# A graph network on one core: batch norm and gate on turned tiles, row norms tile by tile, a second feature buffer, and the start of the build

## The chip, the core and the metric

One core of a Trainium2 chip runs the whole network. The metric is the device time of one execution in microseconds (us). The kernel is written in Bass: every engine has its own program, and the engines meet only at semaphores. TensorE is PE, VectorE is DVE, ScalarE is ACT, GpSimd is POOL and SyncE is SP.

## What is computed

A graph has 3125 nodes with 96 features (`x`) and 100,000 directed edges (`src`, `dst`). Four blocks are added to `x`, each after a layer norm and a ReLU:

```python
h = relu(layernorm(x)); x = x + L0(h)   # two graph convolutions, batch norm and sigmoid between them
h = relu(layernorm(x)); x = x + L1(h)   # two SAGE layers: h @ W_self + mean_of_neighbours(h) @ W_neigh + b
h = relu(layernorm(x)); x = x + L2(h)   # two attention layers with graph norms
h = relu(layernorm(x)); x = x + L3(h)   # degree-normalised sum over edges
# L0
h = graph_conv(h)                        # segment_sum((h * out_norm)[src], dst) * in_norm + bias1
h = sigmoid(batch_norm(h, gamma, beta))  # mean and variance of each feature over the nodes
h = graph_conv(h)                        # same, with bias2
```

## The kernel before, in words

The nodes are 25 tiles of 128 (`NT`), in five groups of five (`G`, `NG`). The kernel first builds the dense adjacency matrix of edge counts, 3200 x 3200 in fp16 (`ADJ`), and every sum over edges is then a matrix product with it.

**The build (`build_adjacency`, L145 to L555).** The edges are sorted by destination. DVE compares sampled destinations with 196 bounds in four slices (L304), PE adds the comparisons up (L399), and DVE makes of them 196 start addresses (L309). Packed edge keys are written to DRAM (L240, L492) and come back as 196 short windows, one DMA each, in seven loads of 8, 16, 28 and four times 36 windows. `load_windows` (L133) reads the addresses from SBUF into registers, four at a time (`QUAD`), and issues the DMAs. SP and ACT each issue half of loads 0 and 1; SP issues all others; a load waits until the buffer it goes to was turned. ACT then issues the loading of `x` (L499, L500). For every four windows (a quad, 49 of them) DVE makes one-hot rows and codes (L331, L338) and ACT a fifth part of the codes (L513, L521). PE multiplies them (L428), ACT stores the counts (L535), and PE adds degrees (L438). PE turns the keys of the next load (L412) after the third-last quad of a load (after the first one of load 0), in its own order between the products, and DVE unpacks them (L317) after the second-last quad (the last one of load 0). Beside the stores of pairs 8 to 32, ACT also takes the sum and the squared deviation of each tile of `x` (L541, L542) for the first layer norm.

**A sum over edges (`pe_aggregate`, L594).** The features stand in `k.Y` as two fp16 halves (high and low, 192 columns). A pass has 625 products of 128 x 128 by 192 columns. The first five output tiles are summed together in five PSUM banks, group of sources by group as `y_ready` comes; then tile after tile with 25 products each, each waiting until its bank was read. `after(j)` puts further PE work behind tile j. DVE reads a bank by adding the two halves (L620).

**The stages around the change, all in `convolutions` and `sage`:** the first layer norm is applied (L730 to L742); the sums of layer 1 (with column sums of `H` by PE, L693); batch norm and gate: mean (L771), centring (L773), squares by ACT (L831), column sums of squares by PE (50 products, L693), scale (L781) and shift (L788) in DVE passes over all tiles, sigmoid by ACT (L836), a multiply by POOL (L816), then the high and low halves (L631, L637); the sums of layer 2; the second layer norm: for each group the sum, mean, centring (L646 to L648), square (L656), sum of squares (L662), and, after the last group, one square root and a pass over all five groups (L669 to L680); the SAGE sums with two turns (L1009, L1010) and two small products (L1018, L1019) after each tile, and the weights scaled by DVE (L917 to L922) before its first bank is read; ReLU by ACT (L982), halves, the second SAGE sums, and the third layer norm in the same way as the second. `attention_weights` turns small weights on PE and DVE between the two stages. `prepare_attention` then turns `H` again (L1269, L1242).

```python
for v, y_ready, w in ((s, k.y_ready, w1), (u, u.y_ready, w2)):     # sage, PE
    after = step(v, w)
    pe_aggregate(k, nc, pe, v, y_ready, 1, ONE, after)
    after(NT)
    after(NT + 1)
```

## Time and profile before

| | before |
|---|---|
| median of 3 runs | 943.2 us (941.07 to 944.72) |
| the profiled execution | 944.32 us, span 942.5 us |
| mean granted clock of TensorE, as a share of full speed | 0.895 |
| PE, PEld, DVE, ACT, POOL busy | 741.9, 674.9, 650.9, 470.6, 10.5 us |
| build, up to the first product of the sums (L598) | 0 to 214.02 us |
| layer 1 sums; batch norm and gate | to 274.49; to 302.69 us |
| layer 2 sums; second layer norm | to 357.87; to 365.82 us |
| SAGE 1 sums; change to SAGE 2; its sums | to 439.76; to 444.71; to 514.17 us |
| first product of the attention's preparation | 523.71 us |
| attention, norms and the last sum, which the change leaves alone | to 942.5 us |

Times are from the start of the span. The span is 1.8 us shorter than the device time of the same execution. A matmul is pipelined, so that its listed duration (250 ns) is longer than the distance to the next one. The clock is the share of full speed that was granted: 1.00 is 2.4 GHz and 0.50 is 1.2 GHz.

### The profile page before, as it was taken

The numbers are of one execution on the slowest core, as the hardware profiler recorded it, in microseconds if no ns is written. First come the engines' busy times: TensorE is split into PE (matmuls) and PEld (weight loads), VectorE is DVE, ScalarE is ACT, GpSimd is POOL, SyncE is SP. The second block draws the span as 40 slices with busy tenths as digits, with TensorE's granted clock in tenths as the row PEclk, the third lists the DMA queues.
The fourth block names the chain that finished last, engine by engine and source line by source line (L and its number), as shares of the span: only waits on it lengthen the run. The fifth ranks groups of instructions, "written<-read, shape, count | busy, mean of one in ns | idle before, by whom it ended". The sixth has DMA issues, their size and how long they took to land. (4 is left out here: it accounts for less than half of the span.)

```text
span 942.5 us, 20574 instructions
## 1 busy us (share of the span) xinstructions
PE 741.9 (79%) x8051; PEld 674.9 (72%) x8051; DVE 650.9 (69%) x1513; ACT 470.6 (50%) x937; POOL 10.5 (1%) x19
## 2 busy tenths in 40 slices
PE   3776888869984996898999749998753999880598
PEld 2555655549974996898999649888642988770498
DVE  5888999974346445334444769998866999889632
ACT  1899999861013002112111559888554988760200
POOL 1000000000002000000000000000000000000000
PEclk8898999998986998999999559999955999995699
DMA  2200000006950000000000210000001489918501
GB/s 74 62 11 11 9 6 2 1 8 239 413 237 1 1 1 1 2 1 2 1 2 11 95 32 16 16 16 2 1 1 33 90 184 190 173 39 229 119 23 31
DMA packets 95284, 56.17 MB, mean 60 GB/s; under 512 B 87960, under 2 KB 89418, under 8 KB 94792
## 3 DMA queue, kind: packets, MB, share of 16 engines
q1 hardware_dynamic: 93982, 52.65, 20.3%
q10 hardware_dynamic: 1194, 2.06, 0.7%
q8 instruction: 69, 1.13, 0.5%
q14 instruction: 39, 0.32, 0.1%
HBM read 9.26 MB, written 24.97 MB: 36 GB/s over the span
## 5 line engine op out<-in xcount | busy, mean ns | idle before, releaser
L598 PE MATMUL banks<-y_sb,adjacency 128*128 128x192 f16 (+1 forms) x2500 | 227.9, 252 | 30.3 <-DVE y_sb L637 30.3
L598 PEld LDWEIGHTS banks<-y_sb,adjacency 128*128 128x128 f16 x2500 | 220.7, 101 | 32.1 <-DVE y_sb L637 30.9
L428 PE MATMUL counts<-hot_code,hot_row 128*128 128x100 f16 (+3 forms) x1568 | 122.1, 219 | 38.1 <-ACT hot_code L521 19.5
L428 PEld LDWEIGHTS counts<-hot_code,hot_row 128*128 128x128 f16 x1568 | 93.5, 101 | 77.8 <-DVE hot_code L338 32.9
L1701 PE MATMUL banks<-loose,y_sb 128*128 128x194 f16 x540 | 101.4, 251 | 0.0
L620 DVE TENSOR_REDUCE h_sb<-banks 128x96 f32<-128x192 f32 x75 | 26.7, 356 | 105.0 <-PE banks L598 67.0
L1700 PE MATMUL banks<-x_sb,gat_masks 128*128 128x194 f16 x420 | 79.8, 252 | 23.3 <-DVE gat_masks L1625 15.3
L338 DVE TENSOR_TENSOR hot_code<-codes_iota,unpacked 128x600 f16<-128x600 f16 x196 | 96.8, 555 | 0.0
L1700 PE MATMUL banks<-x_sb,y_sb 128*128 128x194 f16 x400 | 75.2, 250 | 13.9 <-DVE h_sb L1625 9.9
L535 ACT ACTIVATE adjacency<-counts 128x800 f16<-128x800 f32 x98 | 81.2, 828 | 10.0 <-PE counts L428 9.9
L1673 ACT ACTIVATE gat_masks<-y_sb,node_scalars 128x640 bf16<-128x640 f32 x84 | 68.1, 825 | 29.6 <-PE banks L1701 17.3
L331 DVE TENSOR_TENSOR hot_row<-rows_iota,unpacked 128x2560 f16<-128x2560 f16 x49 | 72.6, 1482 | 7.7 <-PE counts L428 7.6
L1700 PE MATMUL banks<-x_sb,h_sb 128*128 128x194 f16 x430 | 75.8, 247 | 0.8
L1920 PE MATMUL banks<-y_sb,adjacency 128*128 128x192 f16 x625 | 55.0, 252 | 27.0 <-DVE y_sb L637 27.0
L1920 PEld LDWEIGHTS banks<-y_sb,adjacency 128*128 128x128 f16 x625 | 54.4, 100 | 27.9 <-issue 27.5
L978 ACT ACTIVATE loose<-banks 96x256 f32<-96x256 f32 x50 | 19.0, 379 | 110.3 <-PE banks L1010 110.2
L1701 PE MATMUL banks<-loose,h_sb 128*128 128x194 f16 x400 | 72.4, 247 | 0.0
L1673 ACT ACTIVATE y_sb<-y_sb,node_scalars 128x640 bf16<-128x640 f32 x80 | 65.0, 825 | 10.6 <-PE banks L1701 9.7
L1673 ACT ACTIVATE h_sb<-y_sb,node_scalars 128x640 bf16<-128x640 f32 x86 | 68.2, 824 | 0.7 <-PE banks L1701 0.3
L620 DVE TENSOR_REDUCE loose<-banks 128x96 f32<-128x192 f32 x50 | 17.8, 356 | 72.9 <-PE banks L598 72.9
L1700 PEld LDWEIGHTS banks<-x_sb,gat_masks 128*128 128x128 f16 x420 | 41.7, 99 | 29.4 <-DVE gat_masks L1619 16.9
L513 ACT ACTIVATE distance<-codes_iota,negative 128x100 f16<-128x100 f16 x196 | 57.5, 368 | 4.6 <-issue 4.2
(230 smaller groups left out, 1233.8 us busy)
## 6 DMA issues: line engine op xcount, KB each, us to landing
kept_adj<-adjacency SPq DMA_DIRECT2D x5, 4000.0 KB, 32.0
y_sb<-a_dst_rows SPq DMA_DIRECT2D x10, 320.0 KB, 3.5
window_keys<-edge_keys SPq DMA_DIRECT2D x184, 5.0 KB
kept_x<-x_sb SPq DMA_DIRECT2D x1, 1200.0 KB, 4.3
residual<-h_sb SPq DMA_DIRECT2D x5, 240.0 KB, 2.1
loose<-residual SPq DMA_DIRECT2D x1, 1200.0 KB, 5.3
x_sb<-kept_x SPq DMA_DIRECT2D x1, 1200.0 KB, 8.0
out_x<-x_sb SPq DMA_DIRECT2D x4, 240.0 KB
```

The lines of the kernel that those rows point to most:

```text
L331: dve.tensor_tensor(hot_row[:, h, :, :].rearrange("p n (a b) -> p n a b", b=2), rows_iota[:, :].rearrange("p (a b) -> p a b", b=2).unsquee ...
L338: dve.tensor_tensor(hot_codes(h, b).rearrange("p w (a b) -> p w a b", b=2), codes_iota[:, FROM[b]:FROM[b] + WIDE[b]].rearrange("p (a b) -> ...
L428: last = nc.tensor.matmul(counts[:, 2 * (p % HELD) + i, start:end], hot_row[:, q % 2, b * QUAD + w, :], hot_codes(q % 2, b)[:, w, start - ...
L513: nc.scalar.activation(distance[:, q % 2, w, :], codes_iota[:, FROM[-1]:CODES], ACT.Abs, bias=negative[:, load % 2, at:at + 1]).then_inc(d ...
L535: nc.scalar.activation(k.ADJ[:, :, 2 * p * W:2 * (p + 1) * W].rearrange("p t (b o) -> p t b o", o=W), counts_of(2 * (p % HELD), 2), ACT.Co ...
L598: return nc.tensor.matmul(k.ps[:, j % G, 0:cols], k.ADJ[:, i, j * P:(j + 1) * P], k.Y[:, i, 0:cols], start=i == 0, stop=i == NT - 1)
L620: return nc.vector.tensor_reduce(out, k.ps[:, b, 0:ONE].rearrange("p (q f) -> p f q", q=PARTS), axis=AX, op=ALU.add)
L978: nc.scalar.activation(HT[:, j % 2, :], k.ps[0:C, TURNED, 0:2 * P], ACT.Copy).then_inc(v.copied, 1)
L1673: nc.scalar.activation(step_of(x), row[ch % 2], ACT.Relu, bias=k.a_s5[:, i:i + 1], scale=STEEP).then_inc(t.step_ready, 1)
L1700: nc.tensor.matmul(bank[:, 0:2 * BC], over_of(x)[:, q * P:(q + 1) * P], features[0][:, i, :], start=i == 0, stop=False)
L1701: return nc.tensor.matmul(bank[:, 2 * BC:4 * BC], under_of(x)[:, q * P:(q + 1) * P], features[1][:, i, :], start=False, stop=i == NT - 1)
L1920: return nc.tensor.matmul(k.ps[:, j % BANKS, 0:ONE], k.ADJ[:, a * G + i % G, at:at + P], k.Y[:, i, 0:ONE], start=i == 0, stop=i == NT - 1)
```

## The change

In the build: `x` is loaded by SP in six DMAs before the codes are written out; DVE measures each tile with `bn_stats` (five tiles before it turns the counts into start addresses, twenty after); ACT's statistics go; registers are filled up to twelve at a time; ACT issues the last four windows of loads 0 and 1, SP the others; PE multiplies `bound` by itself 60 times before its counting and 45 times after it, into a bank that is overwritten later.

Batch norm: PE turns tiles of `H` between the sums of layer 1, DVE measures the turned tiles in PSUM with `bn_stats`, scale and shift are then columns, and ACT reads the turned tiles and gives the sigmoid of all in one instruction a group; PE turns the gates back, DVE multiplies them with `out_norm`. Row norms: after each tile of the sums DVE takes `bn_stats` and `bn_aggr` of that row tile, and ACT applies the norm and the ReLU with a scale and a bias per row. SAGE 1 reads its features from `k.Y2`, which lies in `k.loose`, and writes those of SAGE 2 to `k.Y` while it sums. The weights of the attention are turned in the batch norm stage. POOL clears the build's semaphores beside the later work.

```diff
+ADDRESSES = 12
+BY_ACT = 4
+STATS_FIRST = 5
+BUSY_FIRST, BUSY_NEXT = 60, 45
 def load_windows(nc, k, d, eng, engine, load, keys, windows, landed):
-    for at in range(0, len(windows), QUAD):
-        some = windows[at:at + QUAD]
+    for at in range(0, len(windows), ADDRESSES):
+        some = windows[at:at + ADDRESSES]
...
+        sp.wait_ge(x_pad, 1)
+        for g in range(NG):
+            full = min((g + 1) * G, NT - 1)
+            sp.dma_start(k.X[:, g * G:full, :], d.x[g * G * P:full * P, :].rearrange("(t p) f -> p t f", p=P)).then_inc(x_in, 16)
+        sp.dma_start(k.X[0:LAST, NT - 1, :], d.x[(NT - 1) * P:N, :]).then_inc(x_in, 16)
         sp.wait_ge(codes_ready, 1)
...
-                         windows[:len(windows) // 2] if load < 2 else windows, window_in[load])
+                         windows[:len(windows) - BY_ACT] if load < 2 else windows, window_in[load])
...
-        dve.wait_ge(count_ready, 1)
-        dve.tensor_scalar(k.start_i[:, :], count_ps, float(STEP), None, ALU.mult).then_inc(starts_ready, 1)
+        dve.wait_ge(x_in, 16 * (NG + 1))
+        for t in range(NT):
+            if t == STATS_FIRST:
+                dve.wait_ge(count_ready, 1)
+                dve.tensor_scalar(k.start_i[:, :], count_ps, float(STEP), None, ALU.mult).then_inc(starts_ready, 1)
+            last = dve.bn_stats(node_stats[:, t, :], k.X[:, t, :])
...
+        pe.wait_ge(iotas, 1)
+        keep_busy(BUSY_FIRST)
         for s in range(SLICES):
...
         last.then_inc(count_ready, 1)
+        keep_busy(BUSY_NEXT)
...
-                chain(nc.scalar.activation(centred, k.X[:, t, :], ACT.Copy, scale=1.0 / C, accum_out=k.mean0[:, t:t + 1]))
-                nc.scalar.activation(squared, k.X[:, t, :], ACT.Square, scale=-1.0, bias=k.mean0[:, t:t + 1],
-                                     accum_out=k.var0[:, t:t + 1]).then_inc(mean_ready, 1)
```

The rest of the core, of `pe_aggregate`, the row norm, `convolutions` and `sage`:

```diff
     for g in range(NG):
         pe.wait_ge(y_ready, g + 1)
         for j in range(G):
+            if g == 0 and drained is not None:
+                pe.wait_ge(drained, NT - G + j + 1)
...
+        if between is not None:
+            between(g)
...
+def row_statistics(nc, k, dve, s, j):
+    dve.wait_ge(s.added, j + 1)
+    if j >= 2:
+        dve.wait_ge(s.row_moments, j - 1)
+    dve.bn_stats(k.row_stats[:, j % 2, :], k.X[:, j, :]).then_inc(s.row_measured, 1)
+def row_moments(nc, k, dve, s, j):
+    dve.wait_ge(s.row_measured, j + 1)
+    dve.bn_aggr(k.moments[:, j, :], k.row_stats[:, j % 2, :]).then_inc(s.row_moments, 1)
+def row_variance(nc, k, dve, s, g):
+    dve.wait_ge(s.row_moments, G * (g + 1))
+    dve.tensor_scalar(group(k.row_dev, g), tiles(k.moments, g)[:, :, 1], LN_EPS, None, ALU.add).then_inc(s.variance, 1)
+def row_scales(nc, k, dve, s, g):
+    dve.wait_ge(s.deviation, g + 1)
+    dve.reciprocal(group(k.row_scale, g), group(k.row_dev, g)).then_inc(s.row_scale, 1)
+    dve.wait_ge(s.row_scale, g + 1)
+    nc.vector.scalar_tensor_tensor(out=group(k.row_shift, g), in0=tiles(k.moments, g)[:, :, 0], scalar=-1.0,
+                                   in1=group(k.row_scale, g), op0=ALU.mult, op1=ALU.mult).then_inc(s.row_shift, 1)
+def act_row_deviation(nc, k, act, s, g):
+    act.wait_ge(s.variance, g + 1)
+    nc.scalar.activation(group(k.row_dev, g), group(k.row_dev, g), ACT.Sqrt).then_inc(s.deviation, 1)
+def act_normalise_rows(nc, k, act, s, g):
+    act.wait_ge(s.row_shift, g + 1)
+    for t in range(g * G, (g + 1) * G):
+        nc.scalar.activation(k.H[:, t, :], k.X[:, t, :], ACT.Relu, scale=k.row_scale[:, t:t + 1],
+                             bias=k.row_shift[:, t:t + 1]).then_inc(s.normal, 1)
...
+BN_TURN_AT = ((8, 0, 5), (13, 5, 10), (18, 10, 12), (22, 12, 16), (23, 16, 20))
+BN_MEASURE_AT = (10, 15, 20, 24)
...
+            for j in range(first, end):
+                nc.vector.scalar_tensor_tensor(out=k.H[:, j, :], in0=k.H[:, j, :], scalar=k.in_norm[:, j:j + 1], in1=bias,
+                                               op0=ALU.mult, op1=ALU.add).then_inc(s.h_ready, 1)
...
+        for n in range(len(BN_MEASURE_AT), NC + 1):
+            measure(nc, k, dve, s.tiles_turned, s.measured, n)
+        dve.wait_ge(s.columns, 2 * 16)
+        dve.wait_ge(s.measured, NC + 1)
+        chain(dve.bn_aggr(k.columns[:, 2:4], k.column_stats.rearrange("p n e -> p (n e)")))
...
         for g in range(NG):
+            dve.wait_ge(s.back, g + 1)
+            dve.tensor_tensor(tiles(k.H, g), back(g), across(group(k.out_norm, g)), ALU.mult).then_inc(u.value, 1)
...
+        for j in range(NT + 6):
+            if j < NT:
+                dve.wait_ge(u.summed, j + 1)
+                add_parts(nc, k, tiles(k.H, j, 1), j % G).then_inc(u.emptied, 1)
+            if 0 <= j - 1 < NT:
+                update(j - 1)
+            if 0 <= j - 2 < NT:
+                row_statistics(nc, k, dve, u, j - 2)
+            if 0 <= j - 3 < NT:
+                row_moments(nc, k, dve, u, j - 3)
+            if (j - 3) % G == G - 1 and 0 <= j - 3 < NT:
+                row_variance(nc, k, dve, u, (j - 3) // G)
+            if (j - 4) % G == G - 1 and 0 <= j - 4 < NT:
+                row_scales(nc, k, dve, u, (j - 4) // G)
+            if (j - 6) % G == G - 1 and 0 <= j - 6 < NT - G:
+                dve_low(nc, k, dve, (j - 6) // G, u.next_high, u.next_y, k.Y2)
+        dve_low(nc, k, dve, NG - 1, u.next_high, u.next_y, k.Y2)
...
+                gate = nc.scalar.activation(gates[:, g % 2, (first - g * G) * P:(first - g * G) * P + z - a],
+                                            flat(k.ps[0:C, :, :])[:, a:z], ACT.Sigmoid, scale=scale, bias=shift)
+        act.preload_act_table(ACT.Sqrt)
         for g in range(NG):
+            act_row_deviation(nc, k, act, u, g)
+            act_normalise_rows(nc, k, act, u, g)
+            act.wait_ge(u.normal, G * (g + 1))
+            act_high(nc, k, g, u.next_high, k.Y2)
...
+            if j == 0:
+                weights()
             if j >= 2:
                 output_1(j - 2)
+            if BIASED_FROM <= j < BIASED_FROM + NG:
+                g = j - BIASED_FROM
...
+                dve.tensor_tensor(tiles(k.X, g), tiles(k.X, g), down(b2[:, :], G), ALU.add).then_inc(s.biased, 1)
+            if j >= 2 * G and j % G == 0:
+                dve_low(nc, k, dve, j // G - 2, s.high, u.y_ready, k.Y)
+        dve_low(nc, k, dve, NG - 1, s.high, u.y_ready, k.Y)
...
+            act.wait_ge(s.relu, g + 1)
+            act_high(nc, k, g, s.high, k.Y)
...
+        act_row_deviation(nc, k, act, u, NG - 1)
+        act_normalise_rows(nc, k, act, u, NG - 1)
...
+        first, second = step(s, w1), step(u, w2)
+        pe_aggregate(k, nc, pe, s, k.Y2, k.y_ready, 1, ONE, first, k.drained)
+        pe_aggregate(k, nc, pe, u, k.Y, u.y_ready, 1, ONE, second, s.emptied, lambda g: first(NT + g) if g < 2 else None)
+        second(NT)
+        second(NT + 1)
```

## Rows read from the trace of the kernel before

**Rows 1.** Stretches by stage: PE, PEld, DVE, ACT, POOL busy, clock, DMA share, GB/s.
```profile
60.00:100.00 40.00, 27.85 (x329) 22.71 (x327) 31.22 (x49) 39.45 (x133) 0.00 (x0) 0.83 0.05 11
100.00:201.60 101.60, 87.58 (x1100) 60.30 (x1097) 101.50 (x159) 92.79 (x213) 0.00 (x0) 1.00 0.02 4
...
274.49:302.69 28.20, 11.48 (x61) 10.82 (x61) 16.11 (x28) 9.39 (x17) 6.20 (x5) 0.68 0.00 0
302.69:357.87 55.18, 55.18 (x628) 54.85 (x629) 25.86 (x52) 3.16 (x6) 0.00 (x0) 0.95 0.01 1
357.87:365.82 7.95, 0.38 (x6) 0.29 (x5) 6.81 (x14) 3.29 (x5) 0.00 (x0) 0.83 0.00 0
365.82:378.40 12.58, 12.58 (x127) 12.37 (x127) 5.40 (x15) 1.81 (x3) 0.00 (x0) 0.84 0.00 1
378.40:384.78 6.38, 3.39 (x23) 2.80 (x22) 4.33 (x17) 1.72 (x5) 0.00 (x0) 0.91 0.01 3
...
439.76:444.71 4.95, 2.39 (x19) 1.92 (x18) 2.09 (x7) 3.20 (x7) 0.00 (x0) 1.00 0.01 3
444.71:456.95 12.24, 12.24 (x127) 12.03 (x127) 6.24 (x11) 1.22 (x3) 0.00 (x0) 0.86 0.00 1
```

**Rows 2.** Groups by line, 31 to 202 us: busy, mean ns, idle before, releaser.
```profile
L331 DVE TENSOR_TENSOR hot_row<-rows_iota,unpacked 128x2560 f16<-128x2560 f16 x47 | 69.7, 1482 | 7.7 <-PE counts L428 7.6
```

**Rows 3.** Timeline of the build's first 32 us: start, duration, idle before.
```profile
8.09 3.62 DVE L304 TENSOR_TENSOR adjacency<-bound,sample 125x1568 f16<-125x1568 f16 x4
...
9.12 5.38 PE L399 MATMUL degree_ps<-adjacency,ones_h 125*1 125x196 f16 x32 [9.12 <-DVE adjacency L304]
...
31.03 0.32 DVE L317 CAST unpacked<-keys_ps 128x160 f16<-128x160 f32 x1 [4.23 <-PE keys_ps L412]
```

**Rows 4.** Two stretches: key writes (8 to 11.6 us) and the load of x.
```profile
8.00:11.60 3.60, 2.48 (x16) 1.95 (x17) 3.60 (x5) 0.00 (x0) 0.00 (x0) 1.00 0.70 222
...
24.00:28.50 4.50, 0.04 (x3) 0.01 (x1) 2.80 (x5) 1.77 (x6) 0.00 (x0) 0.50 0.90 264
```

**Rows 5.** Timeline of window and x issues, and PE's turn of load 2.
```profile
15.70 22.39 SPq L142 DMA_DIRECT2D window_keys<-edge_keys  x40
...
23.45 3.14 ACTq L500 DMA_DIRECT2D x_sb<-in_x  x1
...
40.31 0.51 PE L412 MATMUL keys_ps<-ident,window_keys 56*128 56x56 f32 x5
```

**Rows 6.** Line 137, register loads of four addresses: ns min/median/max.
```profile
L137 SPq TENSOR_LOAD <-start_i x46: 463/554/715, 15.0 to 124.1; - x46
```

**Rows 7.** Groups by line in the sums of layer 1.
```profile
L693 PE MATMUL banks<-h_sb,ones 128*128 128x96 f32 x40 | 5.1, 275 | 0.0
...
L625 DVE SCALAR_TENSOR_TENSOR h_sb<-h_sb,node_scalars 128x480 f32<-128x480 f32 x4 | 2.6, 658 | 0.1
```

**Rows 8.** Three DVE lines of later stages: ns min/median/max.
```profile
L1343 DVE BATCH_NORM_STATS2 node_scalars<-banks x14: 199/678/689, 670.7 to 851.8; 96x6 f32<-96x512 f32 x12, 96x6 f32<-96x53 f32 x2
...
L1814 DVE BATCH_NORM_AGGREGATE node_scalars<-node_scalars x2: 333/333/333, 686.5 to 852.7; 96x2 f32<-96x42 f32 x2
...
L1904 DVE SCALAR_TENSOR_TENSOR x_sb<-h_sb,node_scalars,x_sb x25: 304/308/310, 900.5 to 938.8; 128x96 f32<-128x96 f32 x25
```

**Rows 9.** Timeline of the attention's preparation: turning five tiles, copying them.
```profile
522.89 0.70 ACT L1242 ACTIVATE y_sb<-banks 96x640 f32<-96x640 f32 x1 [1.14 <-PE banks L1269]
...
525.89 1.27 PE L1269 MATMUL banks<-ident,h_sb 128*96 128x128 f32 x5
```

**Rows 10.** Two stretches for the clock: layer 2's first products; attention's preparation.
```profile
302.69:308.70 6.01, 6.01 (x39) 5.68 (x40) 4.78 (x5) 0.73 (x2) 0.00 (x0) 0.52 0.01 3
520.00:540.00 20.00, 16.87 (x76) 15.75 (x76) 15.02 (x35) 12.10 (x30) 0.00 (x0) 0.50 0.20 77
```

**Rows 11.** Timeline: SAGE 2's last output, and the table load behind its norm.
```profile
516.81 0.25 DVE L952 TENSOR_TENSOR x_sb<-x_sb,banks 128x96 f32<-128x96 f32 x1 [0.48 <-PE banks L1019]
...
520.47 1.28 ACT L1205 ACT_TABLE_LOAD   x1
```

More of the change, by code:

```diff
@@ L685, in act_deviation @@
     nc.scalar.activation(k.s2[:, :], k.s1[:, :], ACT.Sqrt).then_inc(deviation, 1)
-def pe_column_sums(nc, k, pe, ready, of, out, g):
-    pe.wait_ge(ready, g + 1)
-    for t in range(g * G, (g + 1) * G):
-        rows = P if t < NT - 1 else LAST
-        last = nc.tensor.matmul(out, k.ones[0:rows, :], of[0:rows, t, :], start=t == 0, stop=t == NT - 1)
-    return last
 def load_rows(sp, loads, done):
@@ new lines, in _ @@
+        pe_aggregate(k, nc, pe, s, k.Y, s.y_ready, 2, ONE + 1, turn)
+        pe.wait_ge(w.loads, 6 * 16)
+        pe.wait_ge(s.emptied, 2 * NT)
+        for n in range(2):
+            nc.tensor.transpose(turned[:, n * C:(n + 1) * C], w_in[:, n, :], k.ident[0:C, 0:C]).then_inc(w.turned, 1)
+            nc.tensor.matmul(logits[:, 2 * n:2 * n + 2], w_in[:, n, :], a_in[:, n, :], start=True, stop=True).then_inc(w.turned, 1)
+        pe.wait_ge(s.h_ready, NT)
+        turn_tiles(nc, k, pe, s.tiles_turned, (NC - 1) * CHUNK, NT)
```

434 lines of the change are left out of this document (207 added, 227 removed).

## The prediction

> **What bounds the kernel now.** I read the busy time by stretches first, cut at the stage borders, then the waits at each border. The kernel is a row of stages with one limit each, so each is costed by itself. In the build from 100 to 201.6 us DVE is busy 101.50 of 101.60 us; from 60 to 100 us it is busy only 31.22 of 40, while ACT is busy 39.45 [rows 1]: there ACT, which also carries the statistics of x, is the limit, and the wait that it causes shows on DVE as 7.6 us before the one-hot rows, ended by PE [rows 2]. In the sums of layer 2 PE is busy all 55.18 us. Between passes PE stands almost still: 11.48 us busy in the 28.20 of batch norm, 0.38 in the 7.95 of the second layer norm, 2.39 in the 4.95 between the SAGE layers [rows 1]. What the change takes out of these gaps is path, microsecond for microsecond; what it adds inside a pass hides under PE as long as DVE keeps up.
>
> One more term lies in the clock. In the first 6.01 us of layer 2's sums 39 products ran, at 0.52 of full speed, that is at the lower level, 1.2 GHz, after PE had stood idle [rows 10]. The other 589 of the pass took 49.17 us [rows 1, 10], 83.5 ns each. Each pass that starts cold thus pays about 2 to 3 us: the first 125 products should take 10.4 us and took 12.58 and 12.24 us in the two SAGE passes [rows 1].
>
> **The build.**
> - *Start.* Counting needs 32 products in 5.38 us, 168 ns each, and ends at 14.50; DVE's comparisons end at 11.71 [rows 3]. 168 ns for 196 columns is the lower clock. The 60 extra products begin at about 1.2 us. Passes that started cold rose after some 4 to 6 us; taking the longer, about 37 run at 163 ns and 23 at 82, so they end at about 9.2, when the first slice comes. Counting at full clock is then bound by DVE: eight products (0.7 us) behind the last slice, 12.4 us. Addresses come 2.0 us earlier. Bounds: 60 products wholly at the lower clock end at 11.0 and counting at 16.4, which is 1.9 us later than now; the best is 2.1 earlier.
> - *x before that.* The five first `bn_stats` stand ahead of the addresses. The row has 0.68 us for 512 columns and 0.20 for 53 [rows 8], so 0.25 for 96 columns, some 0.17 from start to start: 0.9 us from 11.7 to 12.6, hidden but for 0.2. The x data took 4.5 us at 264 GB/s [rows 4]; issued at 3.7 it lands at about 9.6, before DVE asks. Its issue held ACT some 4 us (the second piece alone 3.14 [rows 5]); on SP it ends at about 8, when the codes are ready. The other twenty (3.4 us) end by 16.4, under the wait for the first windows.
> - *The keys* are written from 8.0 to 11.6 us at 222 GB/s [rows 4]. With the tail of x beside them (1.6 us at 264 GB/s) they end near 12.5 to 13, when the addresses come. I take 0 and keep 1 us. The Trainium skill (Trainium Kernel Development and Optimization, Key Constraints) says that DMAs of the SP and ACT queues run on the same engines and interleave, and that a second issuer only saves issue time; by it the x load delays the keys by its share, the 1 us kept above. No row here shows the two together.
> - *Load 1.* DVE waited 4.23 us for its keys [rows 3], since ACT made its first codes only after its windows and the x DMAs. ACT now issues 8 windows instead of 12 and no x. The wait goes.
> - *Load 2 becomes the next late thing.* SP issued 40 windows in 22.39 us, 0.56 each, and PE turned load 2 at 40.31, 2.2 us after the last [rows 5]. Now SP must issue 44 (4, 12, 28). Of the 0.56, 0.14 are the register load of four [rows 6]; with twelve at the same price it is 0.47, so 20.7 us from 13.7: 34.4, turned from 36.6 to 37.1, while DVE, 6.2 us ahead of its old course (unpacking began 1.3 us behind that turn), asks at 35.4. I take a wait of 1.7 us. Bounds: none, and 5 us if a register load costs by the address (44 x 0.56 is 24.6 us, turned from 40.5). The later loads have slack.
> - *ACT's statistics gone:* 40.00 - 31.22 = 8.8 us of idle DVE [rows 1]. ACT without them keeps DVE's pace, as from 100 us on. DVE's seven small operations at the end (0.2 us each) lie in its wait for the last degrees.
>
> Build: 2.0 + 4.2 + 8.8 - 1.7 - 0.3 = **13.0 us** (6 to 15).
>
> **Layer 1 and batch norm.** Forty products for column sums, 5.1 us [rows 7], leave the pass; twenty turns come. Five turns take 1.27 us at the lower clock [rows 9], so about 0.12 each at the full one: 2.4. Gain **2.7** (1 to 3). After the last sum (T) DVE has: reading the bank 0.5, degrees 0.4, `bn_stats` 0.6, scaling and biasing five tiles at 0.31 or less [rows 8] with two reciprocals 2.0; T+3.5. PE turns the last five, 1.1; DVE measures the last three chunks, T+5.3, aggregates (0.33 [rows 8]) and has var by T+6.0; copying the attention weights 0.6, scale and shift 0.7: T+7.3. ACT's table load for the sigmoid (1.28 us, as [rows 11]) ends at T+7.6. Then a pipeline of five groups: gate 0.70 [rows 9], five turns back 1.2, multiply 0.66, high 0.6, low 0.66 (a DVE pass over a group has 0.658 [rows 7]). The latency of a group to its multiply is 2.7 us; ACT's 1.3, DVE's 1.3 and PE's 1.2 a group run beside one another, with the two buffers about 1.65 a group: the last multiply ends at T+17.3, and PE starts there. Now 28.20 [rows 1]: gain **10.9** (7 to 14).
>
> PE enters layer 2 with turns behind it. In the preparation of attention PE was 84% busy with turns and f32 products over 20 us and was granted 0.50 throughout [rows 10], so I count the same cold start as before. The Trainium skill (TensorE: Matmul & The Clock Gate, Part 4, PE-mode transpose) has it that a transpose does not count as PE being busy for the clock; the trace agrees as far as it goes. If the turns did open the clock, the pass would begin warm and the change gain another 3 us, which is in the range.
>
> **Second layer norm.** In the pass a tile costs DVE 0.36 reading, 0.31 adding [rows 8], 0.25 and up to 0.33 for the two statistics and some waits on itself, 1.5 us against PE's 25 x 83.5 ns = 2.09. Hidden. `y_ready` of groups 0 to 2 is there before the pass ends; group 3 comes about 2 us, group 4 about 6.5 us after it (the rest of the loop 3.0, variance, root and scales 1.1, five ACT tiles 1.3, high and low 1.3). PE needs them after 6.3 and 8.4 us of SAGE 1's first products. So PE never stops: 7.95 + 12.58 us [rows 1] become 10.4: **10.1** (6 to 10.1).
>
> **SAGE.** DVE reads the first bank before it scales the weights, not after (part of the 6.38 us in which PE is busy 3.39 [rows 1]): **0.9** (0 to 2.5). Between the layers the products of the last two tiles stay (2.39), the wait for them hides under groups 0 and 1: 4.95 + 12.24 become 2.4 + 10.4, **4.4** (2.5 to 4.5); group 4's halves come 9.4 us after the last sum and are needed at 11. DVE's bias passes, five of 0.66, and its statistics fit in 2.73 us a tile.
>
> **Third layer norm.** The last output ends at 517.06 [rows 11]. Behind it: statistics and moments of the last two tiles 1.0, variance, root, scales 1.1, five ACT tiles 1.3, then the table load for the exponential (1.28 [rows 11]), no longer hidden under DVE: the first copy at 521.7 instead of 522.89 [rows 9]: **1.2** (0 to 3).
>
> **Sum:** 13.0 + 2.7 + 10.9 + 10.1 + 0.9 + 4.4 + 1.2 = 43.2 us. The profiled execution took 944.3, so 901.1; it lies 1.1 above the median of the runs, so **900.0 us** as a median. From 523.7 us on nothing changes.
>
> **Rivals.**
> 1. *The windows or the clock spoil the start.* Register loads that cost by the address (3.3 us more) and counting at the lower clock (3.9 more): 903 to 907 us. For it: SP's issue was just in time for load 2 before [rows 5], and PE is blocked in its own order meanwhile. Chance 0.15.
> 2. *A norm's tail becomes the new wait.* If the self-waits of DVE double the tail behind layer 2 to 13 us, group 4 is late by 4.6; if batch norm's groups follow one another unpipelined (2.7 + 1.3 each instead of 1.65), it gives back up to 5: 905 to 909. Chance 0.11.
> 3. *The relief of ACT does nothing:* DVE's idle from 60 to 100 us was ended by PE [rows 2], whose clock was 0.83 there [rows 1]. If the slow stretches of PE were the cause and come again, 8.8 us stay: 909. Against it: from 100 us on, without statistics, the clock is 1.00. Chance 0.06.
> 4. *Better:* layer 2 and SAGE 1's steps at full clock, 3 to 5 us more: 896. Chance 0.07.
> 5. *Slower.* From layer 2 to the end of SAGE PE now runs some 205 us without a pause. If the clock were then cut to the lower level, each product would cost 154 ns, not 83.5 [rows 1, 10]. The gain is eaten once 43.2 / 0.0705 = 613 products run so, about one pass of 625; two passes so give 901 + 88 = 989 us. Against it: from 100 to 201.6 us the clock is 1.00 with PE 86% busy, and in layer 2 nothing lowers it behind the start. Chance 0.03.
>
> **Chances.** The forecast has 0.58. Everything but rival 5 is faster by much more than 0.5%, which is about what a measurement can tell from no change: faster 0.95, same 0.02 (several bounds at their bad end together), slower 0.03. The forecast's own terms spread by some 6 us; the range reaches over rivals 1 to 4: 891 to 912.
>
> **What would show it.** Right: addresses near 12.9 us, a DVE wait of 1 to 2 us before load 2 near 36, almost none from 60 to 100, the last one-hot codes near 188; 17 us between layer 1's last sum and layer 2's first; no gap in PE before SAGE 1 and SAGE 2; five ACT tiles behind the last output. Wrong: a PE gap before SAGE 1's fourth or fifth group, DVE waits at every window load, counting products at 168 ns, or a clock under 1.00 in the middle of the long run of passes.

## The result and the profile after

The changed kernel took **896.7 us** (median of 4 runs, 895.97 to 899.46) against 943.3 for the kernel before (4 runs beside it, 941.07 to 944.72): ratio 0.9515, 95% interval 0.9499 to 0.9531. The profiled execution took 897.3 us, its span is 895.5. Forecast: 900.0, range 891 to 912. Forecast and range held; what follows is about the terms behind them.

First the stages, cut at the borders of the kernel after. Columns: from and to, length, busy time and count for PE, PEld (weight loads), DVE, ACT and POOL, PE's granted clock, DMA share, GB/s.

```profile
core 0: us, PE busy (x) PEld busy (x) DVE busy (x) ACT busy (x) POOL busy (x), PEclk, DMA share, GB/s
60.00:100.00 40.00, 34.63 (x427) 24.69 (x425) 39.93 (x65) 34.98 (x80) 0.00 (x0) 0.96 0.05 12
...
200.89:257.67 56.78, 56.74 (x645) 56.27 (x645) 23.74 (x98) 2.85 (x8) 0.00 (x0) 0.98 0.91 367
257.67:274.23 16.56, 6.46 (x36) 4.90 (x37) 11.04 (x36) 8.12 (x14) 0.00 (x0) 0.62 0.00 0
274.23:328.50 54.27, 54.27 (x625) 54.02 (x626) 25.93 (x108) 10.87 (x26) 0.00 (x0) 0.96 0.01 2
328.50:338.89 10.39, 10.39 (x129) 10.39 (x127) 5.08 (x21) 4.54 (x12) 0.00 (x0) 1.00 0.01 2
338.89:344.31 5.42, 3.25 (x25) 2.72 (x24) 3.81 (x15) 1.62 (x5) 0.00 (x0) 0.93 0.00 0
```

DVE is now busy 39.93 of the 40 us from 60 to 100, where it was 31.22 [rows 1]. Batch norm is 16.56 us instead of 28.20. Between layer 2 and SAGE 1 there is no row for a gap, because PE has none: its 129 operations fill all 10.39 us.

The start, from the timeline of PE and DVE (start, length, engine, line; in brackets the idle time before and its releaser):

```profile
1.20 7.34 PE L420 MATMUL keys_ps<-bound 128*128 128x196 f16 x60 [1.20 <-POOL bound L269]
9.61 3.50 PE L427 MATMUL degree_ps<-adjacency,ones_h 125*1 125x196 f16 x32 [1.07 <-DVE adjacency L312]
```

```profile
8.59 3.62 DVE L312 TENSOR_TENSOR adjacency<-bound,sample 125x1568 f16<-125x1568 f16 x4
12.13 0.89 DVE L321 BATCH_NORM_STATS2 node_stats<-x_sb 128x6 f32<-128x96 f32 x5
13.14 0.35 DVE L320 TENSOR_SCALAR start_i<-degree_ps 1x196 int32<-1x196 f32 x1
...
25.03 0.31 DVE L330 CAST unpacked<-keys_ps 128x160 f16<-128x160 f32 x1
...
38.50 0.45 DVE L330 CAST unpacked<-keys_ps 128x280 f16<-128x280 f32 x1 [2.85 <-PE keys_ps L441]
```

Counting takes 3.50 us instead of 5.38 [rows 3] and keeps up with DVE's slices. (Two later runs without extra products counted in 4.70 and 4.75 us, so some 0.6 us of the old 5.38 belong to that one trace.) Addresses come at 13.14 (forecast near 12.9): DVE got the destinations 0.5 us later than before, so its slices ended at 12.2. Load 1 is unpacked without a wait; load 2 waits 2.85 us (forecast 1 to 2). The last one-hot codes end at 188.8 (forecast near 188).

Layer 2's last statistics behind its last sum, and the join to SAGE 1, from the timeline of ACT and of DVE:

```profile
331.69 0.21 ACT L688 ACTIVATE mean<-mean 128x5 f32<-128x5 f32 x1 [1.32 <-DVE mean L673]
332.35 1.90 ACT L695 ACTIVATE h_sb<-x_sb,node_scalars 128x96 f32<-128x96 f32 x5 [0.45 <-DVE node_scalars L681]
334.28 0.60 ACT L645 ACTIVATE loose<-h_sb 128x480 f16<-128x480 f32 x1
```

```profile
334.91 0.66 DVE L651 SCALAR_TENSOR_TENSOR loose<-h_sb,loose 128x480 f16<-128x480 f32 x1 [2.60 <-ACT loose L645]
```

Group 4 is ready at 335.57, 7.1 us behind the end of layer 2's sums (328.50); SAGE 1's first products, which begin at 328.57, need it 8.4 us in. The tail was forecast at 6.5 (five ACT tiles at 1.3; they take 1.90). It fits with 1.3 us to spare.

The whole gain, stage by stage. Each length is the distance between the same two events in the two traces (to within 0.1 us). Layer 2's sums end here where DVE begins to read their last bank (357.89 and 328.77 us), and a group of sums ends where PE's next small operation begins, so some lengths differ by up to 0.3 us from those of the windows above:

| Stage | before | after | gain | forecast |
|---|---|---|---|---|
| start to first sum product | 214.02 | 200.89 | 13.1 | 13.0 |
| sums of layer 1 | 60.47 | 56.78 | 3.7 | 2.7 |
| batch norm | 28.20 | 16.56 | 11.6 | 10.9 |
| sums of layer 2 | 55.20 | 54.54 | 0.7 | 0 |
| second layer norm, SAGE 1's group products | 20.33 | 10.12 | 10.2 | 10.1 |
| SAGE 1's weights and first steps | 6.56 | 5.42 | 1.1 | 0.9 |
| SAGE 1 from there to the end of SAGE 2's group products | 72.01 | 66.86 | 5.2 | 4.4 |
| SAGE 2, third norm, to the first attention product | 66.92 | 65.98 | 0.9 | 1.2 |
| the rest | 418.8 | 418.4 | 0.4 | 0 |
| span | 942.5 | 895.5 | 47.0 | 43.2 |

### The profile page after: what moved, and what is told of

Same layout as the page of the kernel before. It is cut to its first block and busy times, and to the rows that moved or that the text cites. A ratio compares the mean times of both kernels' runs of the same rounds, so it can differ in the third digit from the quotient of the medians.

```text
span 895.5 us, 20798 instructions
## 1 busy us (share of the span) xinstructions
PE 736.5 (82%) x8106; PEld 666.6 (74%) x8106; DVE 640.1 (71%) x1662; ACT 467.5 (52%) x881; POOL 4.3 (0%) x14
## 5 line engine op out<-in xcount | busy, mean ns | idle before, releaser
L614 PE MATMUL banks<-y_sb,adjacency 128*128 128x192 f16 (+1 forms) x1875 | 165.9, 249 | 8.5 <-DVE y_sb L651 7.8
L614 PEld LDWEIGHTS banks<-y_sb,adjacency 128*128 128x128 f16 x1875 | 161.6, 99 | 9.4 <-DVE y_sb L651 7.9
L457 PEld LDWEIGHTS counts<-hot_code,hot_row 128*128 128x128 f16 x1568 | 91.6, 100 | 65.0 <-DVE hot_code L351 40.3
L1999 PEld LDWEIGHTS banks<-y_sb,adjacency 128*128 128x128 f16 x625 | 54.4, 100 | 27.8 <-issue 27.4
L1116 ACT ACTIVATE y_sb<-banks 96x256 f32<-96x256 f32 x50 | 19.1, 382 | 97.5 <-PE banks L1148 97.5
L640 DVE TENSOR_REDUCE y_sb<-banks 128x96 f32<-128x192 f32 x50 | 17.9, 357 | 66.2 <-PE banks L614 66.2
L539 ACT ACTIVATE distance<-codes_iota,negative 128x100 f16<-128x100 f16 x196 | 57.4, 367 | 11.5 <-DVE negative L336 11.5
```

What stands on the lines that cost most here:

```text
L457: last = nc.tensor.matmul(counts[:, 2 * (p % HELD) + i, start:end], hot_row[:, q % 2, b * QUAD + w, :], hot_codes(q % 2, b)[:, w, start - ...
L539: nc.scalar.activation(distance[:, q % 2, w, :], codes_iota[:, FROM[-1]:CODES], ACT.Abs, bias=negative[:, load % 2, at:at + 1]).then_inc(d ...
L614: return nc.tensor.matmul(k.ps[:, j % G, 0:cols], k.ADJ[:, i, j * P:(j + 1) * P], y[:, i, 0:cols], start=i == 0, stop=i == NT - 1)
L640: return nc.vector.tensor_reduce(out, k.ps[:, b, 0:ONE].rearrange("p (q f) -> p f q", q=PARTS), axis=AX, op=ALU.add)
L1116: nc.scalar.activation(HT[:, j % 2, :], k.ps[0:C, TURNED, 0:2 * P], ACT.Copy).then_inc(v.copied, 1)
L1999: return nc.tensor.matmul(k.ps[:, j % BANKS, 0:ONE], k.ADJ[:, a * G + i % G, at:at + P], k.Y[:, i, 0:ONE], start=i == 0, stop=i == NT - 1)
```

## Experiments

All but one are edits of the changed kernel. Each ratio is against the kernel before, run beside it; the changed kernel's is 0.9515, and 0.001 is 0.94 us. A *turn* is a transpose on PE, and the *relief* of ACT is that its statistics of `x` are gone. "Theory" and "rival" are those of the expectation above each result.

One place changes by itself from trace to trace and stands in several of the totals below. In SAGE 1's first steps PE works thinly, and in the changed kernel its granted clock was 0.54 from 343.80 to 347.20 us; the first 25 products behind them took 3.33 us. They took 3.3 to 3.4 us in five of the twelve traces of this kernel and its edits, and 2.1 us in the seven others, two of which are edited in the build alone. So 1.3 us of a difference between two profiled executions can come from there.

**ACT's statistics put back.** DVE keeps its own; ACT's results go unused.

```diff
+            t = p - 8
...
+            if 0 <= t < NT:
+                chain(nc.scalar.activation(centred, k.X[:, t, :], ACT.Copy, scale=1.0 / C, accum_out=sums[:, 0, t:t + 1]))
+                chain(nc.scalar.activation(squared, k.X[:, t, :], ACT.Square, scale=-1.0, bias=sums[:, 0, t:t + 1],
+                                           accum_out=sums[:, 1, t:t + 1]))
```

> The changed kernel, with ACT's two operations for each tile of x put back beside the stores of pairs 8 to 32; their results go unused, DVE's own statistics stay. Theory: in that stretch ACT was what the build waited for, and its relief brought 8.8 us. Then ACT is busy all the time from some 60 to 100 us, DVE stands idle there for 8 to 9 us with PE named as releaser, and the kernel takes 905 us. Rival: the slow clock of PE was the cause and went by itself; then DVE stays busy, and the time is within 1 us of 896.7.

912.0 us, ratio 0.9672 (0.9656 to 0.9688): 15 us, not 8.8, and 13.0 of them stand ahead of the first sum product. A window of this kernel and its waits of DVE (total us, times, longest):

```profile
40.00:100.00 60.00, 42.40 (x480) 32.98 (x478) 47.38 (x74) 58.39 (x190) 0.00 (x0) 0.83 0.04 10
```

```profile
DVE hot_row L347 <- PE counts L460: 11.6, 9, 2.4
DVE unpacked L333 <- PE keys_ps L444: 4.6, 3, 2.3
```

ACT is busy 58.39 of 60 us and DVE loses 11.6 us to it by way of PE, 7.6 in the kernel before [rows 2]. The first sum product comes at 213.93, where the kernel before had 214.02. With ACT's work back, the other edits of the build bring 0.1 us: they let DVE reach the stretch in which ACT is the limit earlier, and it waits there longer. Theory right in kind, wrong in size.

**The kernel before, without ACT's statistics.** Row means and variances are constants in their place. The lines that go:

```diff
...
-                chain(nc.scalar.activation(centred, k.X[:, t, :], ACT.Copy, scale=1.0 / C, accum_out=k.mean0[:, t:t + 1]))
-                nc.scalar.activation(squared, k.X[:, t, :], ACT.Square, scale=-1.0, bias=k.mean0[:, t:t + 1],
-                                     accum_out=k.var0[:, t:t + 1]).then_inc(mean_ready, 1)
...
```

> The kernel before the change without ACT's two operations per tile of x in the build; mean and variance of the rows are constants in their place, nothing else differs. With those operations put back into the changed kernel its first sum product came at 213.93 us, against 214.02 before the change and 200.89 after: the earlier start was worth 0.1 us without the relief of ACT. This run asks what the relief is worth without the earlier start. Theory: only the 7.6 us that DVE waited for ACT by way of PE, and the end of that wait, so the first sum product comes near 206 and the kernel takes 935.5 us. Rival: the relief is worth as much here as in the changed kernel, 13 us: 201, and 930 us.

931.3 us, ratio 0.9877 (0.9860 to 0.9893); first sum product at 204.12. Waits of DVE in this build:

```profile
DVE unpacked L317 <- PE keys_ps L414: 9.2, 2, 4.7
DVE out_deg L356 <- PE degree_ps L440: 2.8, 1, 2.8
```

The 7.6 us in front of the one-hot rows are gone, the waits for keys stay: 9.9 us for the relief alone, 0.1 for the other edits alone, 13.1 for both. On top of the relief the other edits thus bring 3.2 us, which is the 3.1 us by which load 2 was unpacked earlier (38.50 instead of 41.59). Both prices named beforehand miss: it lies between 8 and 13. Most of the other 2 us of the total go with the clock: layer 1 and batch norm took 87.4 us instead of 88.7 with no edit there, and the granted clock of layer 1's first 5.9 us was 0.69 instead of 0.52.

**Four addresses to a register load** instead of twelve (`ADDRESSES = 4`).

> The changed kernel with four addresses to a register load instead of twelve. Theory: SP's issue of the 44 windows ahead of load 2's end sets DVE's wait before load 2 (2.85 us now, windows at 0.498 us each). At 0.56 each they end 2.7 us later, the wait grows to 5.6 us and the kernel takes 899.4 us. Rival: a register load costs by the address, so nothing is saved by loading twelve at once: the windows stay near 0.50 each, the wait stays, 896.7 us.

898.9 us, ratio 0.9528 (0.9512 to 0.9544). The unpacking of load 2:

```profile
40.94 0.45 DVE L330 CAST unpacked<-keys_ps 128x280 f16<-128x280 f32 x1 [5.19 <-PE keys_ps L441]
```

2.4 us later than with twelve, first sum product 203.32 instead of 200.89: the theory. SP issued the 44 windows in 24.52 us instead of 22.03. The interval of the runs alone overlaps that of the changed kernel; the trace decides.

**A smaller load 2.**

```diff
-LOADS = (8, 16, 28, 36, 36, 36, 36)
+LOADS = (8, 16, 20, 32, 40, 40, 40)
```

> The changed kernel with loads of 8, 16, 20, 32, 40, 40 and 40 windows instead of 8, 16, 28 and four of 36. Theory: load 2's keys are late because 44 windows of SP go ahead of them. With 36 ahead they are issued by 32.2 us and turned from about 34, before DVE asks at 35.65: the wait of 2.85 us goes and no later load is late, 893.9 us. Rival 1: what comes late is PE's own place for the turn, between products of the quads; then 1 us or more of wait stays, 895 to 896 us. Rival 2: load 3 comes late in its place (its last window is issued near 48 us, asked for near 52), 896 us or more.

894.6 us, ratio 0.9479 (0.9464 to 0.9495): 2.1 us less by the medians, 3.4 by the ratios, 1.4 by the spans. No load but the first is waited for:

```profile
DVE unpacked L330 <- PE keys_ps L441: 1.5, 1, 1.5
```

The term is right, and both rivals fall. This execution lost 1.1 us of it at the start. Its extra products became fast earlier (25 of them from 4.00 to 6.00 us, 16 in the changed kernel) and ended at 7.81, PE stood 1.77 us, and counting took 4.58 us, not 3.50, at a granted clock of 0.65:

```profile
1.20 6.61 PE L420 MATMUL keys_ps<-bound 128*128 128x196 f16 x60 [1.20 <-POOL bound L269]
9.58 4.58 PE L427 MATMUL degree_ps<-adjacency,ones_h 125*1 125x196 f16 x32 [1.77 <-DVE adjacency L312]
```

**No extra products** (`BUSY_FIRST, BUSY_NEXT = 0, 0`).

> The changed kernel without the 60 and 45 extra products that PE runs before and after counting. Theory: they bring the clock up before counting. Without them the 32 counting products take 168 ns each as before the change, the addresses come near 15.0 us instead of 13.14, and everything behind is 1.5 to 1.9 us later: 898.4 us; the first quads run at the lower clock somewhat longer, which DVE's pace hides. Rival: the key writes, not the addresses, release the windows; then the addresses are later and the first window is not, 896.7 us.

899.3 us, ratio 0.9536 (0.9520 to 0.9552). Counting took 4.70 us, 147 ns each, addresses came at 14.08 and the first sum product at 201.76, 0.9 us later. The products help, by half of what was expected: by the trace 0.9 us, by the runs 2 with an uncertainty of about the same size. In this trace DVE's slices also began 0.36 us earlier (8.23, not 8.59), so from an equal start it would be 1.3. The help isn't certain either: of the eleven traces with extra products ahead of the count, nine counted in 3.5 us, and two, where PE stood 1.70 and 1.77 us behind them, in 4.59 and 4.58.

**One buffer between layer 2 and SAGE 1.** DVE's low halves go behind its last tile, ACT's high halves behind layer 2's last sum, and SAGE 1 writes the second buffer.

```diff
-            if (j - 6) % G == G - 1 and 0 <= j - 6 < NT - G:
-                dve_low(nc, k, dve, (j - 6) // G, u.next_high, u.next_y, k.Y2)
-        dve_low(nc, k, dve, NG - 1, u.next_high, u.next_y, k.Y2)
+        for g in range(NG):
+            dve_low(nc, k, dve, g, u.next_high, u.next_y, k.Y)
...
+            if g == NG - 1:
+                act.wait_ge(u.summed, NT)
+                for n in range(NG - 1):
...
+                    act_high(nc, k, n, u.next_high, k.Y)
             act_row_deviation(nc, k, act, u, g)
...
-            act_high(nc, k, g, u.next_high, k.Y2)
+        act_high(nc, k, NG - 1, u.next_high, k.Y)
```

> The changed kernel with the halves of layer 2's normalised rows written to the buffer that layer 2's own sums read, so only behind its last product; the statistics tile by tile and the normalising by ACT stay. (SAGE 1 writes the second buffer in its place.) Theory: most of the 10.1 us came from measuring under the sums, not from the buffer: PE then stands for one high and one low half, 1.3 to 1.5 us, and the later groups follow faster than it needs them: 898 us, or up to 899.6 if the pause lowers its clock. Rival: the second buffer carries the term; then some 8 us come back, 905 us.

900.7 us, ratio 0.9556 (0.9540 to 0.9572): 3.9 us more than the changed kernel, between theory and rival. PE in this kernel:

```profile
325.83 2.75 PE L614 MATMUL banks<-y_sb,adjacency 128*128 128x192 f16 x31
332.68 12.23 PE L614 MATMUL banks<-y_sb,adjacency 128*128 128x192 f16 x125 [4.10 <-DVE y_sb L651]
```

The pause is 4.10 us, not 1.4: the edit put the first low half behind group 4's statistics in DVE's order (they end at 332.0; the first high half was there 2 us before). Behind the pause the group products took 12.23 us instead of 10.4, so the stage is 6.0 us longer (16.13 us, not 10.12). Of this 1.3 us came back in SAGE 1's first 25 steady products, which took 2.10 us here and 3.33 in the changed kernel. So this run bounds the buffer's part of the stage's 10.2 us at 6.0 from above; at least 4.2 come from measuring under the sums. What a better order would give was not tried.

**SAGE 1 waits for all five groups.**

```diff
+        pe.wait_ge(k.y_ready, NG)
         pe_aggregate(k, nc, pe, s, k.Y2, k.y_ready, 1, ONE, first, k.drained)
```

> The changed kernel, but SAGE 1's first product waits until all five groups of rows are ready. Theory: the tail of the norm ends 7.1 us behind layer 2's last sum, so PE stands 7.1 us, and its clock then falls: the group phase takes 12.5 us instead of 10.4. In all some 9.2 us, 906 us. Rival: the pause alone counts, the clock comes back at once, 903.8 us.

906.4 us, ratio 0.9617 (0.9601 to 0.9633): 9.6 us, the theory.

```profile
336.32 12.75 PE L614 MATMUL banks<-loose,adjacency 128*128 128x192 f16 x125 [6.88 <-DVE loose L651]
```

Pause 6.88 us, then 125 products in 12.75 us instead of 10.4: the theory in both parts. In its own stage a pause in PE cost more than its length: this one 9.3 us, the one of 4.10 us in the run before 6.0. In this profiled execution (905.2 us, the fastest of the four) 1.3 us came back in SAGE 1's first steps, as above.

**SAGE 1's last two steps ahead of SAGE 2's products.**

```diff
+        first(NT)
+        first(NT + 1)
-        pe_aggregate(k, nc, pe, u, k.Y, u.y_ready, 1, ONE, second, s.emptied, lambda g: first(NT + g) if g < 2 else None)
+        pe_aggregate(k, nc, pe, u, k.Y, u.y_ready, 1, ONE, second, s.emptied)
```

> The changed kernel with SAGE 1's last two steps (turn, copy, product) ahead of SAGE 2's first product, as before the change, and not behind its first two groups. Theory: PE then waits for the reading, scaling, turning and copying of these tiles, 2 to 2.5 us, and may pay up to 2 us of lower clock: 899.2 us (899 to 901). Rival: group 4's halves, some 9.4 us behind the last sum, bind in either order, so part of the wait is hidden again: 897 us.

897.5 us, ratio 0.9524 (0.9506 to 0.9542): no difference that the runs can tell. The trace of this kernel:

```profile
399.97 0.39 PE L1157 MATMUL banks<-y_sb 96*128 96x96 f32 x2
400.84 0.46 PE L1156 MATMUL banks<-y_sb 96*128 96x96 f32 x2 [0.48 <-ACT y_sb L1116]
401.14 0.39 PE L1157 MATMUL banks<-y_sb 96*128 96x96 f32 x2
401.36 10.60 PE L614 MATMUL banks<-y_sb,adjacency 128*128 128x192 f16 x125
```

From the last steady step to the end of SAGE 2's group products it is 13.21 us (398.59 to 411.80), and 12.16 in the changed kernel (399.01 to 411.17), whose last two steps stand inside the pass: 1.05 us. The pause of 0.48 us is so short that the clock stays up: the 125 products take 10.4 us. Before the change the same place had 4.95 us and a cold pass behind it [rows 1]. So about 1 of the 5.2 us is the order of the steps, and the rest is PE not waiting for normalised rows. The rival's figure came out, though not by group 4, whose halves bound in neither order.

**Extra products, and extra turns, in batch norm.** 35 products of 128 columns before the last turns, 55 behind them, 10 behind each group turned back; then the same places with 18, 28 and 5 turns of an f32 tile.

```diff
+        extra_products(nc, k, 35, 4)
         pe.wait_ge(s.h_ready, NT)
         turn_tiles(nc, k, pe, s.tiles_turned, (NC - 1) * CHUNK, NT)
+        extra_products(nc, k, 55, 4)
...
             last.then_inc(s.back, 1)
+            extra_products(nc, k, 10, 5 if g == 0 else 6)
```

> The changed kernel with 140 extra products of 128 columns in batch norm, where PE waits: 35 before the last turns, 55 behind them, 10 behind each group turned back, into banks that nobody reads at the time. Theory: PE's clock follows its products; it stays up through batch norm, so layer 2's sums start at full clock (they ran their first 4.7 us at half, which costs 2.3 us) and the turns take half as long: 3 us less, 893.7 us. Rival: the clock falls all the same or the extra products hold the turns back: 896.7 us or up to 1 us more.

> The same places as in the run with 140 extra products, but turns of a 128x128 f32 tile, 71 of them, about the same time of PE at the upper clock. Theory: turns do not bring or hold the clock; it falls in batch norm as now, layer 2 starts at half clock, 896.7 us, and up to 1.5 us more because at the lower clock the extra turns take twice as long and stand before the useful ones. Rival: any work of PE does it, 893.7 us as with products.

Products: 892.4 us, ratio 0.9469 (0.9455 to 0.9482). Turns: 893.4 us, ratio 0.9476 (0.9461 to 0.9490). The runs can't tell them apart. The windows of batch norm and of layer 2's first 10 us, with products:

```profile
259.00:274.10 15.10, 12.11 (x176) 11.09 (x176) 10.87 (x36) 8.10 (x13) 0.00 (x0) 1.00 0.00 1
274.10:284.00 9.90, 9.87 (x119) 9.87 (x120) 4.59 (x6) 1.89 (x2) 0.00 (x0) 1.00 0.01 2
```

and with turns:

```profile
259.00:274.10 15.10, 12.49 (x114) 11.07 (x114) 10.84 (x33) 8.79 (x15) 0.00 (x0) 1.00 0.00 0
274.10:284.00 9.90, 9.90 (x121) 9.90 (x119) 4.70 (x9) 1.18 (x1) 0.00 (x0) 1.00 0.01 2
```

In both, batch norm takes 15.3 us instead of 16.6 and layer 2's sums 52.2 instead of 54.3. The clock stays at 1.00 throughout. The window with turns also holds the first 0.70 us of layer 2, which begins at 273.40; from 258.70 to there PE was busy 12.09 of 14.70 us with nothing but turns and two small products of the attention weights, at 1.00. In both, SAGE 1's first 25 steady products took 2.1 us instead of 3.33, another 1.3 us, which came without an edit in other runs too. The theory for products holds; that turns don't hold the clock is refuted.

**Extra products before layer 1 (75) and before the preparation of attention (75).**

> The changed kernel with 75 extra products of 128 columns before layer 1's sums, where PE stood 7.8 us, and 75 before the first product of the first preparation of attention, where it stood 4.9 us. Theory: layer 1 starts at full clock, 1.5 us less; the preparation, in which PE was busy 13.9 of 17 us at 0.50 of its clock, runs at full clock as far as it holds, 3 us less: 892.2 us. Rival: in the preparation, f32 products and turns let the clock fall within some us, and 75 products at the way down stand in the way: only layer 1's 1.5 us come, 895.2 us.

891.3 us, ratio 0.9457 (0.9444 to 0.9471), 5.4 us less than the changed kernel: more than the theory's 4.5. Layer 1's sums took 55.5 us instead of 56.8. SAGE 1's first 25 steady products took 2.07 us instead of 3.33, which is none of the edit's. The preparation, first before this edit, then with it:

```profile
477.15:495.00 17.85, 14.78 (x66) 13.88 (x66) 11.13 (x28) 10.54 (x29) 0.00 (x0) 0.50 0.02 5
507.23:514.40 7.17, 6.53 (x40) 5.47 (x41) 4.82 (x13) 2.57 (x5) 0.00 (x0) 0.52 0.01 2
```

```profile
474.79:483.50 8.71, 6.54 (x55) 6.12 (x55) 5.91 (x18) 6.72 (x19) 0.00 (x0) 0.98 0.03 8
483.50:507.40 23.90, 9.31 (x49) 7.46 (x50) 16.49 (x46) 11.11 (x23) 0.00 (x0) 0.51 0.10 31
507.40:515.00 7.60, 7.60 (x94) 7.60 (x92) 7.51 (x19) 7.59 (x12) 0.00 (x0) 1.00 0.00 0
```

Four of the five groups of the preparation now run at the upper clock, and from its first product to the turn of the destination row (L1391) it takes 11.5 us, not 15.4.

**All together,** with the smaller load 2:

> All that gained, in one kernel: the smaller load 2 (2.1 us by its run), the extra products in batch norm (4.3), those before layer 1, 60 now, and before the preparation of attention (5.5 together); and, not run before: 12 more before counting, 15 in the first steps of SAGE 1, and 60 in the waits of both preparations' ends and 38 ahead of each attention's first product, which now runs its first 7 us at half clock. Theory: the gains lie in different stages and add up: 11.9 us, 1.3 for SAGE 1's step, 2.5 for each attention: 878.5 us. Rival 1: the clock is not up at the attentions' first product, since PE's work in the waits before is too thin to raise it: 884 us. Rival 2: extra work behind extra work brings the clock down elsewhere or holds up the useful products: 886 us or more.

884.0 us, ratio 0.9369 (0.9355 to 0.9383): the best version, 12.7 us below the changed kernel and 58.9 below the one before. It is rival 1's figure: the gains already measured added up to about what is seen, the new ones brought about nothing. SAGE 1's first steps fell to half clock here, which they didn't in the runs whose gains were added. PE at the start of the first attention:

```profile
489.07 1.67 PE L613 MATMUL banks<-ident_h 128*128 128x128 f16 x14
495.54 4.23 PE L613 MATMUL banks<-ident_h 128*128 128x128 f16 x38 [4.80 <-issue]
499.57 0.37 PE L1796 MATMUL banks<-x_sb,gat_masks 128*128 128x194 f16 x1
```

```profile
479.70:500.20 20.50, 13.31 (x111) 12.09 (x110) 15.38 (x45) 9.73 (x18) 0.00 (x0) 0.50 0.12 36
500.20:505.00 4.80, 4.80 (x60) 4.79 (x59) 2.02 (x6) 2.74 (x4) 0.00 (x0) 1.00 0.01 3
```

PE stands 4.80 us between the two kernel parts with no releaser named, starts the 38 extra products when the first masks are nearly due, and the useful ones come 11.0 us behind the last product of the preparation (488.56) instead of 7.4: 3.6 us late. From there on they run at the upper clock 0.6 us in, instead of 7.2; that gives back about what the delay took. In SAGE 1 the 15 products moved the half-clock stretch from 343.8 to 336.3 us (344.31 is where the changed kernel's steady steps begin, 337.3 here) and did not remove it.

## Why the forecast held, and where its steps were off

(In brackets: forecast; measured, in us.) The median of 896.7 is close to rival 4's 896, but that rival's mechanism, layer 2 and SAGE 1's steps at full clock, isn't in this trace: both fell to half clock in part. The forecast's own mechanisms are there; no step of them failed, and what was off are sizes. No run takes apart batch norm's 11.6 us, the earlier reading of SAGE 1's first bank or the third norm; these rest on the reading of the trace.

- **The build (13.0; 13.1)** came out by a sum of which no term stands alone. "Start 2.0, load 1's wait 4.2, ACT's relief 8.8, load 2 -1.7" took each from its own row of the trace before and added them. The runs show them nested: without the relief the rest is worth 0.1 us, alone the relief 9.9, both 13.1. The sum held because the change had both, and its closeness is luck: in the forecast's own terms the start and the loads were to bring 4.2 us and the relief 8.8, and the runs show 3.2 and 9.9. Of its terms, the start was 1.4 (destinations 0.5 us late; DVE's slices began at 8.09 and 8.29 us in the two traces without the early load of x and from 8.23 to 8.79 in the twelve with it, so the spread between traces is as large as the difference), and load 2's wait 2.85 instead of 1.7. The step that was off is "with twelve at the same price": a register load of twelve took 1.00 us (median), one of four 0.55 [rows 6], so a window cost 0.498 us instead of 0.47, and 44 of them reached from 14.3 to 36.2. Within its bounds.
- **Rival 3** (the relief does nothing) is refuted by two runs. **Rival 1** (windows or clock spoil the start) didn't occur; its clock half is real in small: counting took 3.5 us in nine traces with extra products and 4.58 and 4.59 in two.
- **Layer 1 (2.7; 3.7)** and **layer 2 (0; 0.7)** are sizes, and what was mis-sized is "I count the same cold start as before", which for layer 1 was taken without being said. Layer 1 ran 2.91 us at the lower clock instead of 5.98, layer 2 4.67 instead of 6.11. At half speed such a stretch costs half its length: 1.5 and 0.7 us. The column sums that left layer 1 were taken at their listed 5.1 us [rows 7]; ten of them held the pass for 1.12 us, so all forty for 4.5. Four turns in the pass cost 0.43 us, 0.48 by the forecast. The lengths change from kernel to kernel by themselves: the kernel before without ACT's statistics gained 0.9 and 0.4 us in the same two stages, unedited, and in the nine runs that leave layer 1 as it is in the changed kernel it took 0.1 to 1.6 us longer. So I don't count this part as a gain of the edit.
- **Batch norm (10.9; 11.6).** The path was as written: variance at T+5.6 behind the last sum T (forecast 6.0), the sigmoid's table in at T+7.1 (7.6), PE's first product at T+16.6 (17.3). The pipeline of five groups took 9.4 us, 9.7 forecast.
- **Second layer norm (10.1; 10.2).** PE never stopped. The run that makes it wait gives the term back almost whole, 9.3 us in the stage: 6.9 of pause and 2.4 of clock. The forecast had it as 7.95 of pause and 2.2 of clock. **Rival 2** had its mechanism right (the tail 0.6 longer than forecast), but 1.3 us of slack were left.
- **SAGE 1 to 2 (4.4; 5.2)** right. Of the extra, 0.4 us lie in the join: from the last steady step to the end of the group products it took 12.2 us and not the 12.8 counted (2.4 for the last steps and 10.4). The other 0.4 lie in the steady steps, 2.70 us a tile instead of 2.73. The 2.70 go with the buffer: where SAGE 1 reads `k.Y` and SAGE 2 the second buffer (the run with one buffer), SAGE 1's steps take 2.73 and SAGE 2's 2.70.
- **Third norm (1.2; 0.9)** within bounds.
- **The Trainium skill's rule** (TensorE: Matmul & The Clock Gate, Part 4, PE-mode transpose), taken into the forecast for layer 2's start, says that a transpose doesn't count as PE being busy. In the run that fills the pauses with turns the clock stayed at 1.00 for 14.7 us and through the start of the next pass, as with products; the measurement decides. The forecast came out at that place, since the clock did fall in batch norm (0.97 up to 261.8 us, 0.50 from there on). It fell behind PE's pauses of 0.6 and 2.3 us and stayed down through those of 3.8 and 1.6; filled with turns or products, they left it up, so the pauses did it and not the turning.
- **The other rule of the Trainium skill** (Trainium Kernel Development and Optimization, Key Constraints: the SP and ACT queues' DMAs share engines and interleave) might explain the destinations' 0.5 us; no run here shows that it does, and the spread between traces is as large. Beyond it nothing of the 1 us kept for the keys was seen: the first window was issued at 14.28, behind the addresses.
- **Rival 4** (warm passes, 3 to 5 us) is what the runs with extra work in batch norm had: 1.3 us in batch norm, 2.1 in layer 2 and 1.3 in SAGE 1's first steps, the last not by that work alone. **Rival 5** (the clock is cut in the long run) is refuted: nothing lowered it from 347.2 to 476 us. A clock under 1.00 in the long run of passes was named as a sign of being wrong, and there is one, 3.4 us at 0.54 in SAGE 1's first steps; but it stood at the same place before the change (0.79 and 0.65 from 382.00 to 388.00 us), and it is a start behind thin work and no cut of a busy engine.

## What to carry to other kernels

Gains read from separate waits on the same engine are not a sum until each is tried without the others: an earlier start in front of a stretch that another engine limits is worth nothing until that engine is relieved. Look for what the last group's tail needs and what the consumer's first groups take: the two numbers, 7.1 and 8.4 us here, decide whether a norm costs its length or nothing. And count a pause of TensorE at its length plus the cold start behind it (6.9 us cost 9.3 and 4.1 cost 6.0 here, 0.5 no more than itself); where the pause can't go, cheap work in it buys the cold start back. Before a microsecond or two is laid to an edit, compare the stages that it doesn't touch: here they moved by up to 1.6 us by themselves.

## What the runs showed of the hardware

- Turns of f32 tiles held TensorE's clock as products did (1.00 over 14.7 us, PE busy 12.09). Whether they can also raise it isn't shown: in the preparation of attention, entered at the lower clock, PE was busy 14.78 of 17.85 us with turns and f32 products and stayed at 0.50. Entered at the upper clock the same work ran 8.7 us at 0.98. In these two kernels the level that held there was the one at which the stretch was entered.
- Loading twelve addresses to registers at once instead of four took a window from 0.56 to 0.50 us; the load itself took 1.00 us for twelve and 0.55 for four.
- Extra products behind a pause of 4.8 us with no named releaser at the start of a kernel part did not begin when the engine fell idle: they ended about 3.6 us after the useful work could have begun. ACT and DVE stood in the same place, for 3.4 and 5.0 us; why is open.
- The record of the granted clock reads 1.00 all through the count before the change, though its products of 196 columns took 168 ns each; in the run with the smaller load 2, 25 such products fit into 2.00 us (80 ns each) at a recorded 1.00. There the level is told by the products' lengths and not by the record.
